# Input projections of two batches in three float32r products instead of one column-tiled float32 product

## The reference, cut to what matters

```python
x = x + ssm_mixer(layernorm(x))               # RMS norm, W_in, conv, scan, gate, W_out
x = x + cross_attention(layernorm(x), ctx)    # 32 query heads, 8 key heads, head size 16
x = x + moe(layernorm(x))                     # shared expert, 16 experts, top 2
```

```python
xn = x * rsqrt(mean(x * x) + EPS) * w_norm
proj = einsum('bld,td->blt', xn, W_in)        # 2576 columns: z, xi, dt, B, C
...
scores = einsum('bkgsd,bktd->bkgst', qh, kh) / 4
weights = softmax(scores)
```

## Time and profile before

| | |
|---|---|
| runs | 1196.25, 1197.2, 1201.25 us; median 1197.2 us |
| profiled execution | 1196.14 us, its span 1194.3 us |
| granted TensorE clock | 0.993 of full speed |
| busy in the span | PE 1132.4, DVE 771.3, ACT 565.6, POOL 454.0 us |
| exponential of slot 36, of slot 78 | 289.39, 422.64 us |
| exponential of slot 100, of slot 142 | 488.10, 621.49 us |

### The profile page before, as it was taken

The page is one execution under the profiler, slowest core; times in us unless marked ns, Lnnn a source line. Parts: engine busy times, 40 slices in busy tenths (PEclk is TensorE's granted clock), DMA queues, the critical chain, the costliest instruction groups (busy, mean ns, idle before and its releaser), DMA issues. The chain is left out here.

```text
span 1194.3 us, 31724 instructions
## 1 busy us (share of the span) xinstructions
PE 1132.4 (95%) x13187; PEld 638.5 (53%) x13188; DVE 771.3 (65%) x1254; ACT 565.6 (47%) x811; POOL 454.0 (38%) x549
## 2 busy tenths in 40 slices
PE   5979898999999999999999999999989999999996
PEld 4857655445555544544645554444444555565654
DVE  5646766756787665668675787877748555555553
ACT  5745453433555443545444365555533344444443
POOL 5487444311321330122022122101101477777776
PEclk9999998999999999999999999999999999999999
DMA  5444757104373200356410135310205876788740
GB/s 130 116 114 116 156 134 131 53 3 122 73 164 85 74 25 23 83 120 115 93 41 16 68 82 91 79 38 3 73 19 183 229 158 133 191 236 245 186 83 13
DMA packets 119606, 122.27 MB, mean 102 GB/s; under 512 B 25472, under 2 KB 84992, under 8 KB 119344
## 3 DMA queue, kind: packets, MB, share of 16 engines
q1 hardware_dynamic: 101744, 98.59, 32.4%
q0 software_dynamic: 17008, 21.16, 9.4%
q10 hardware_dynamic: 720, 0.61, 0.2%
HBM read 94.63 MB, written 40.77 MB: 113 GB/s over the span
## 5 line engine op out<-in xcount | busy, mean ns | idle before, releaser
L832 DVE TENSOR_REDUCE mx<-ps_m 128x2 f32<-128x1024 f32 x256 | 312.9, 1222 | 200.0 <-PE ps_m L1242 172.7
L1079 ACT ACTIVATE prob<-ps_s 128x1024 f32<-128x1024 f32 x256 | 262.1, 1024 | 320.8 <-PE ps_s L1242 298.5
L1242 PE MATMUL acc<-xnT,wring 128*32 128x512 f32 x1664 | 219.2, 592 | 0.0
L2181 PE MATMUL ps_gu<-ring,xgT 128*128 x376 | 176.9, 593 | 1.5 <-DVE xgT L1856 1.0
L1791 POOL DMA_INDIRECT out<-y,dest x92 | 146.6, 1594 | 60.7 <-issue 35.5
L1242 PE MATMUL ps_s<-q_stack,k_stack 99*32 99x512 bf16 x1936 | 153.1, 381 | 4.2 <-ACT prob L1079 3.6
L1242 PE MATMUL ps_m<-k_stack,q_stack 96*32 96x512 bf16 x1840 | 144.3, 380 | 9.7 <-DVE mx L832 8.2
L1476 PEld LDWEIGHTS ps_o<-prob,values 128*32 128x32 f32 x4096 | 116.7, 110 | 44.8 <-issue 39.1
L1476 PE MATMUL ps_o<-prob,values 128*32 128x128 f32 x4096 | 140.1, 275 | 0.0
L1242 PEld LDWEIGHTS ps_m<-k_stack,q_stack 96*32 96x32 bf16 x1840 | 52.0, 96 | 119.2 <-issue 66.0
L1974 DVE TENSOR_TENSOR down_low<-ring,down_high 128x1024 fp32r<-128x1024 f32 x46 | 56.4, 1226 | 66.9 <-ACT down_high L2028 49.8
(11 more groups left out here) (340 smaller groups left out, 1712.5 us busy)
## 6 DMA issues: line engine op xcount, KB each, us to landing
ring<-in_w_experts SPq DMA_DIRECT2D x96, 256.0 KB
wring<-in_w_in SPq DMA_DIRECT2D x80, 256.0 KB, 4.1
q_stack<-part_rows SPq DMA_DIRECT2D x96, 128.0 KB, 4.7
wring<-in_w_out SPq DMA_DIRECT2D x32, 256.0 KB, 3.3
part_rows<-part SPq DMA_DIRECT2D x20, 384.0 KB, 4.3
out<-x SPq DMA_DIRECT2D x4, 1024.0 KB, 5.7
xt<-in_x SPq DMA_DIRECT2D x14, 256.0 KB, 4.4
k_stack<-part_rows SPq DMA_DIRECT2D x48, 64.0 KB, 3.3
```

Of the source, the lines that this page charges most:

```text
L832: nc.vector.tensor_reduce(mx[:, n % G, 2 * u:2 * u + 2], ps_m[:, :, :], AX.X, ALU.max).then_inc(s_max, 1)
L1079: nc.scalar.activation(prob[:, slot % PROB, :, :], ps_s[:, :, :], ACT.Exp, scale=SCALE).then_inc(s_exp, 1)
L1242: ins = nc.tensor.matmul(dst[c:c + 32, :], stationary[:, c:c + 32], moving, start=start, stop=stop, tile_position=(0, c))
L2181: ins = nc.tensor.matmul(ps_gu[p][:, :], xgT[:, p, k * P:(k + 1) * P], weights(own)[:, k * 2 * F:(k + 1) * 2 * F], start=(k == 0), stop=(k ...
```

## The change

`SPLIT_BATCHES` goes, and the projections of all four batches run as `split_product`; `QUIET = 2` keeps what else depended on the batch (how silu is made, the order of blocks and banks). The output projection of batches 1 to 3 and the heads-to-inner product stay as they are.

- The ring's places follow from one list: a block in pieces (`halved`) takes two units of ten, a whole one takes one. In the projections of batches 2 and 3 a block is now loaded 5 blocks ahead instead of 10.
- 40 more blocks (20 in each of batches 2 and 3) get `high_weights` on ScalarE and `low_weights` on GpSimd. The high piece falls on odd slots, the low one on even slots; the first block of the batch is cut at m = 50 and 51 of the batch before.
- Tokens of batches 2 and 3 are taken out of PSUM as before by one VectorE instruction, now into the memory of the low piece; ScalarE rounds them one slot later (`high_tokens`) and GpSimd subtracts one slot after that (`low_tokens`), 4 of each per batch.
- `project_steps` makes two float32 products per quarter and token block in batches 2 and 3, instead of one.
- `tiled[0]` is false in all attention slots with m < 42 of a mixer batch. So in slots 36 to 77 and 100 to 141 scores, maxima and `outputs` are whole products as well. Slots 14 to 35, 78 to 99 and those from 142 on stay tiled.

```diff
-    SPLIT_BATCHES = 2
+    QUIET = 2
...
+        xnT_raw = over("xnT_raw", [P, KD, SEQ], F32)
...
+        def halved(v):
+            return v < BLOCKS or v % BLOCKS < GROUPS - 1
+        STARTS = [0] + list(itertools.accumulate(1 + halved(v) for v in range(BLOCKS * B)))
+        BLOCK_OF = [v for v in range(BLOCKS * B) for _ in range(1 + halved(v))]
+        def unit(v):
+            return (STARTS[v + 1] - 1) % UNITS_IN_RING
+        def before_in_ring(v):
+            return BLOCK_OF[STARTS[v + 1] - 1 - UNITS_IN_RING]
...
-        HIGH_AT = {w: freed_at(w - RING) + 3 for w in range(RING, FIRST_RAW)} | {23: 42, 24: 49}
+        LATER = range(RING, BLOCKS * B)
+        HIGH_AT = {v: freed_at(before_in_ring(v)) + 3 for v in LATER if halved(v)} | {23: 42, 24: 49} | {
+            BLOCKS * b: PERIOD * (b - 1) + 50 for b in range(2, B)}
...
             def freed(b, w):
                 done, value, _ = consumed(b, w)
                 sp.wait_ge(done, value)
+                for v in LATER:
+                    if before_in_ring(v) == BLOCKS * b + w:
+                        load_raw(v)
...
+            def low_tokens(b, j):
+                cols = slice(j * P, (j + 1) * P)
+                pool.wait_ge(s_xhigh, TB * b + j + 1)
+                nc.gpsimd.tensor_tensor(xnT_low[:, :, cols], xnT_raw[:, :, cols], xnT_high[:, :, cols], ALU.subtract
+                                        ).then_inc(s_xnT, 1)
...
+            def high_tokens(b, j):
+                cols = slice(j * P, (j + 1) * P)
+                act.wait_ge(s_xraw, TB * (b - QUIET) + j + 1)
+                nc.scalar.activation(xnT_high[:, :, cols], xnT_raw[:, :, cols], ACT.Copy).then_inc(s_xhigh, 1)
...
-                        whole = [xnT[:, k, cols]]
-                        if b < SPLIT_BATCHES:
-                            whole = [xnT_high[:, k, cols].bitcast(F32), xnT_low[:, k, cols].bitcast(F32)]
+                        both = [xnT_high[:, k, cols].bitcast(F32), xnT_low[:, k, cols].bitcast(F32)]
...
-                if b < SPLIT_BATCHES:
-                    ins = split_product(bank(b, n), [w[:, cols] for w in weights],
-                                        (xnT_high[:, k, :], xnT_low[:, k, :]), start=(k == 0), stop=(k == KD - 1))
-                else:
-                    ins = product(bank(b, n), weights[:, cols], xnT[:, k, :], start=(k == 0), stop=(k == KD - 1))
+                ins = split_product(bank(b, n), [w[:, cols] for w in weights],
+                                    (xnT_high[:, k, :], xnT_low[:, k, :]), start=(k == 0), stop=(k == KD - 1))
...
-                tiled[0] = slot >= FULL_SLOTS
+                tiled[0] = slot >= 0 and (b >= B or m >= 2 * GROUPS)
```

More of the change, by code:

```diff
@@ L3 @@
+import itertools
 from contextlib import ExitStack
@@ L272, in stream_phase, with landing, landed, halves @@
         BLOCKS = GROUPS - 1 + KI
[L273 to L283, removed]
+        UNITS_IN_RING = 2 * RING
+        def halved(v):
[4 more added lines that the diff above has]
+            return (STARTS[v + 1] - 1) % UNITS_IN_RING
+        def landing(v):
+            return s_raw[unit(v)], 16 * [unit(a) for a in range(v + 1)].count(unit(v))
+        def landed(v):
+            return ring[:, unit(v), :]
+        def before_in_ring(v):
+            return BLOCK_OF[STARTS[v + 1] - 1 - UNITS_IN_RING]
+        def halves(v):
+            place = STARTS[v] % UNITS_IN_RING // 2
+            return pieces[:, place, 0, :], pieces[:, place, 1, :]
+        def count_halved(v):
+            return sum(halved(a) for a in range(v + 1))
         def out_order(b):
@@ L658, in _ @@
                         deviations(b + 1)
-                for w in range(RING, FIRST_RAW):
-                    if LOW_AT[w] == slot + LEAD:
-                        low_weights(w)
+                for v in LOW_AT:
+                    if LOW_AT[v] == slot + LEAD:
+                        low_weights(v)
+                if QUIET <= b + 1 < B and m - 2 in EVAC_AT[b]:
+                    low_tokens(b + 1, EVAC_AT[b].index(m - 2))
                 if u == 5 and 0 <= n - 1 < N - 1:
@@ L1216, in _ @@
                             high_gated(b, i)
-                for w in range(RING, FIRST_RAW):
-                    if HIGH_AT[w] == slot + LEAD:
-                        high_weights(w)
+                for v in HIGH_AT:
+                    if HIGH_AT[v] == slot + LEAD:
+                        high_weights(v)
+                if QUIET <= b + 1 < B and m - 1 in EVAC_AT[b]:
+                    high_tokens(b + 1, EVAC_AT[b].index(m - 1))
                 if b == 0 and m in CUT_AT and CUT_AT.index(m) % 2 == 0:
                     piece_of_heads(CUT_AT.index(m))
-                if b + 1 < SPLIT_BATCHES and m in EVAC_AT[b]:
+                if b + 1 < QUIET and m in EVAC_AT[b]:
                     evacuate_high(b + 1, EVAC_AT[b].index(m))
@@ L1352, in project_steps @@
                         cols = slice(j * P, (j + 1) * P)
-                        whole = [xnT[:, k, cols]]
-                        if b < SPLIT_BATCHES:
-                            whole = [xnT_high[:, k, cols].bitcast(F32), xnT_low[:, k, cols].bitcast(F32)]
-                        for h, rows in enumerate(whole):
+                        both = [xnT_high[:, k, cols].bitcast(F32), xnT_low[:, k, cols].bitcast(F32)]
+                        for h, rows in enumerate(both):
                             ins = nc.tensor.matmul(bank(b, 0)[32 * j:32 * j + 32, 0:P], wdt[:, k, :], rows,
                                                    start=(k == 0 and h == 0),
-                                                   stop=(k == KD - 1 and h == len(whole) - 1),
+                                                   stop=(k == KD - 1 and h == 1),
                                                    tile_position=(0, 32 * j))
```

71 lines of the change are left out of this document (26 added, 45 removed).

## The result

The changed kernel takes 1188.6 us (median of 6 runs, 1186.3 to 1191.7), the kernel before 1197.0 us beside it (6 runs, 1196.3 to 1201.3). The ratio is 0.9926, 95% interval 0.9909 to 0.9943: 0.74% faster. The forecast was 1185.0 us, with a range of 1180 to 1193. So some 8.5 us came of the 12 that were forecast.

What follows compares the result with a forecast made beforehand. TensorE was taken to bound the projecting stretches. Per batch 8.4 - 0.6 - 0.2 = 7.6 us, of which 6.0 taken to arrive; 12 us for two batches, from 1197.2 to 1185 us, range 1180 to 1193.

Steps and rivals of the forecast that it cites:

- The products: Projecting slots: even ones gain 0.27 us, odd ones 0.08, four sets of query transposes 0.36 each; 8.4 us per batch.
- between 0 and 1.0 + 0.2 us; I take 0.6: TensorE's doubled small products in project_steps, partly hidden in slots short of work: 0.6 us lost per batch.
- The 0.2 us for slot m = 1: Odd slot m = 1 pays 0.19 us for the tiling change without saving anything, in each batch.
- I take nothing for these: ScalarE's added copies and GpSimd's subtractions fit in free time: no cost; bound 15 us per batch if none were hidden.
- How much of it arrives: Batch 1 against batch 2, slots 8 to 13: 62% of the saving arrives; 4.7 to 7.6 us per batch, 6.0 taken.
- B, VectorE taking over: VectorE becomes the bound where xi blocks are, slots 48 to 63 keep their length: 1192 us; chance 0.14.
- C, a late load: A late load stops ScalarE and lowers the clock, 8.1 us per batch: 1201 us; chance 0.08.
- D, GpSimd holding up VectorE: Silu multiplies of xi blocks wait for GpSimd's low pieces: 1203 us, or 1192 if half of it comes; chance 0.08.
- the 0.19 of the prediction: Odd slots: going from whole products to column tiles and back costs TensorE 0.19 us each time.

Runs made afterwards that it cites:

- short low pieces: Changed kernel with GpSimd's low pieces of weights in batches 2 and 3 cut to 16 of 512 columns, TensorE using high pieces instead: 1181.7 us, ratio 0.9884.

## Why the forecast was right, and what was off in it

**The products: right.** 8.4 us per batch stood for 40 slots. Even slots measured 2.29 us (2.31 forecast), odd ones 3.39 (3.38), slots 48 to 63 a gain of 3.59 (3.5). With short low pieces the 40 slots from 38 to 77 took 120.22 us, 8.24 less than before.

**project_steps: right in kind, too small.** The step "between 0 and 1.0 + 0.2 us; I take 0.6" measured 1.18, its upper end: slot 36 took 1.75 us before and takes 2.93. Of this 0.94 is the second product, shown by leaving it out, and 0.23 goes with the whole products around. The 0.2 us for slot m = 1 were right (3.04 to 3.22 us). The reason given for less, that slots m = 0 and 1 are short of work, was true and useless: the free time came behind the added work.

**"I take nothing for these": the step that failed.** ScalarE's copies did lie in free time. GpSimd's 24 subtractions were summed against its own idle time (34 us into 100 free), and there they fitted. What they cost was the time of VectorE's instructions beside them, and in slots 74 and 138 that of GpSimd's csb behind them, in three places in batch 2 and two in batch 3: 3.37 + 1.82 = 5.2 us, shown by shortening them and, at 3.4 us of these, by moving them. The sum with both terms measured is 8.4 - 0.2 - 1.18 - 3.37 = 3.65 us for batch 2 and 8.4 - 0.2 - 1.18 - 1.82 = 5.2 for batch 3, 8.85 in all; the stretches measured 8.7.

**"How much of it arrives": wrong, and it helped.** The factor of 0.62 was to stand for an unknown loss spread over all slots. There was none such: most slots gained in full, and a few lost much. 12 us came from it, where the step without it would have given 15.2. That the forecast came so near was luck in this part: the factor stood in place of a loss that had not been found and that it does not measure. The slots that it was read from show so. Slots 8 to 11 and 13 of batch 1 are 0.28, 0.08, 0.27, 0.08 and 0.21 us shorter than slots 72 to 75 and 77, and only slot 12 is longer, 2.94 us for 2.67. VectorE's timeline there, batch 1:

```profile
212.61 0.55 DVE L708 TENSOR_SCALAR x<-xt,keep 128x512 f32<-128x512 f32 x1
213.07 0.54 DVE L710 TENSOR_SCALAR xt<-xt,mv,rstd 128x512 f32<-128x512 f32 x1
213.64 1.23 DVE L832 TENSOR_REDUCE mx<-ps_m 128x2 f32<-128x1024 f32 x1
```

No GpSimd subtraction runs beside these. The two residual steps stand in front of the maximum, whose product in ps_m had begun at 212.27; the same slot of batch 2 has none. That they cost the missing 0.4 us is read from these rows and not shown by a run, but in the changed kernel slot 76, without them, takes 2.34 us. The prediction named these two steps as what set the comparison apart, and still scaled every slot by it; in batch 2 just such steps, lengthened, became the largest loss.

**The rivals.** B, VectorE taking over: no; slots 48 to 63 have their full gain, although VectorE is busy there for 43.6 of 46.66 us. C, a late load: no; ScalarE's copies of weights wait for no load in batch 2 and for 1.4 us in all in batch 3, and the granted clock is 1.00 in both stretches. D, GpSimd holding up VectorE: the mechanism was there, in 5.2 us in all, but not where it was looked for. The silu multiplies took 0.68 us as before, but no subtraction ran beside any of them in slots 48 to 63 or 112 to 127, so whether one would lengthen them isn't shown. The taps, which read one operand from PSUM, had one beside them for up to 2.1 of their 2.31 us for three, and took 2.31 before too. Normalising, the residual and the scans were lengthened. The Trainium skill, SBUF — State Buffer, Who interferes with whom, names in the same list as two-operand instructions copies, casts and `tensor_scalar` where they can run in a mode with two ports. The rows here agree: 0.54 us became 1.50, and 0.18 became 1.23, on TENSOR_SCALAR instructions with one tensor operand in SBUF. It also says that whoever comes first has the port for its whole length; the 2.20 us of the subtraction behind a scan agree. The prediction had taken only the first half of the rule, and so looked at the wrong instructions.

**The mode changes.** The Trainium skill, TensorEngine Tiling (Array Packing), Key Properties, has a change of mode drain TensorE. Here a change to column tiles and back cost 0.24 us among float32 products and 0.29 where tiles stand between pieces, by the lengths of whole slots; the 0.19 of the prediction was a little low, and the odd slots measured with it (3.38) were right since they were read as a whole.

## What to carry to other kernels

Work that is put on an idle engine has to be summed twice: against that engine's free time, and against the instructions of the other of the two, VectorE or GpSimd, that happen to run beside it. List these for VectorE and GpSimd by time, not by totals; moving eight of 20 subtractions per batch by a few slots, and one group of products by half a slot, took back 6.3 of the 7.1 us lost to the subtractions and to the doubled products (5.2 + 2 x 0.94). Put added work behind the product that another engine waits for, not in front of it. A saving that falls short in sum is better looked for slot by slot: here most slots gained in full and four places lost nearly all of what was missing. A factor from a comparison should be taken apart in the same way before it is applied: this one came from one slot of six.

## What the runs showed of the hardware

- A VectorE instruction over 128x4 elements (0.18 us) took 1.23 us beside a GpSimd subtraction of 1.27 us, and 0.65 us in the kernel before beside an addition of 0.73 us: in these rows the loss is set by the other's length, not by its own size.
- Three convolution taps with one operand in PSUM took 2.31 us with a GpSimd subtraction beside them for 2.1 us, and 2.31 without.
- In single executions of several kernels, the kernel before among them, the granted clock fell within slot 15 or 165, while TensorE was busy (4.07 of 5.31 us in the row above; 2.59 of 3.83 where the clock stayed at 1.00), and cost 1.5 us each time; the same kernel had the fall in one execution and not in another. What sets it off was not found. It belongs into the reading of any gain under 0.3% here.
